# Token slots of an expert dealt out over eight groups of partitions, and a start at slot 4 in every second turn

## What is computed

```
x  = x + relu(segment_sum(edge_weight * (layernorm(x) @ W)[src], dst) + bias)
xt = layernorm(x)                                 # the input of the experts
scores = sigmoid(xt @ Wg.T + bg); w, idx = top_k(scores, 2); w = w / w.sum()
nx = layernorm(xt)
h  = silu(nx @ (gamma*W1) + b1') * (nx @ (gamma*W3) + b3')   # per expert, 64 of them
y  = sum over the token's two experts of w * (h @ W2 + b2)
z  = a small shared expert on nx
x  = x + y + z
```

## Time and profile before

| what | value |
|---|---|
| median of 3 runs | 431.51 us (431.15 to 432.36) |
| profiled execution, its own time | 432.0 us |
| its span in the profile | 430.2 us |
| PE busy | 398.4 us |
| plain transfers (q1) | 120.45 MB |
| transfers with an index per row (q0) | 8.28 MB |

### The profile page before, as it was taken

One profiled execution on the slowest core, in us unless ns is written; L12 is line 12 of the kernel. 1 busy time (PEld: TensorE's weight loads), 2 busy tenths in 40 slices (PEclk: granted clock), 3 DMA queues, 4 the chain that ended last, 5 costly groups with the idle time before them and its releaser, 6 DMA issues.

```text
span 430.2 us, 6405 instructions
## 1 busy us (share of the span) xinstructions
PE 398.4 (93%) x1898; PEld 207.4 (48%) x1899; DVE 213.2 (50%) x696; ACT 156.9 (36%) x387; POOL 174.1 (40%) x275
## 2 busy tenths in 40 slices
PE   6988999999999998999999999999898969897985
PEld 5656777756556557443443443443333433343331
DVE  8899998225666776633323323423313232123337
ACT  8767787322322220232332332332312321131232
POOL 2769996314655576523423323323312132121100
PEclk9999999999999998999999999999989998899999
DMA  7899971400002764499999999999999999999578
GB/s 254 211 335 408 406 287 47 137 31 26 25 25 63 281 232 146 151 402 410 400 407 405 410 406 407 406 407 406 405 406 409 405 408 404 406 399 406 231 273 325
DMA packets 44022, 129.15 MB, mean 300 GB/s; under 512 B 8054, under 2 KB 9270, under 8 KB 43858
## 3 DMA queue, kind: packets, MB, share of 16 engines
q1 hardware_dynamic: 38242, 120.45, 73.1%
q0 software_dynamic: 5744, 8.28, 5.4%
HBM read 119.64 MB, written 17.85 MB: 320 GB/s over the span
## 4 chain that ended last, share of the span: by engine, by line
PE 80%; issue 6%; DVE 5%; POOL 4%; DMA 3%; ACT 1%; SPq 1%; DVEq 0%; POOLq 0%; ACTq 0%
PE bank L1479 27%; PE bank L1342 13%; PE bank L1509 12%; PE bank L1501 5%; PE bank L1291 4%; PE bank L1467 4%; PE bank L1264 3%; DMA w<-totals 2%; PE bank L1236 2%; PE bank L1330 2%; PE bank L1363 2%; POOL M L502 1%; POOL AT L502 1%; PE bank L1351 1%; PE bank L1412 1%
## 5 line engine op out<-in xcount | busy, mean ns | idle before, releaser
L1136 DVE SCALAR_TENSOR_TENSOR osl<-bank,b13T,osl 128x64 f32<-128x64 f32 x128 | 27.5, 277 | 155.3 <-ACT osl L736 155.3
L1479 PE MATMUL bank<-w,xhT 128*64 128x512 f32 x368 | 87.6, 618 | 11.5 <-issue 11.5
L729 ACT COPY xh<-bank 128x512 f32<-128x512 f32 x33 | 19.4, 586 | 138.0 <-PE bank L1479 131.9
L1342 PE MATMUL bank<-HW,AT 128*128 128x512 f32 x128 | 58.2, 593 | 0.0
L1479 PEld LDWEIGHTS bank<-w,xhT 128*64 128x64 f32 x368 | 26.5, 141 | 56.5 <-issue 54.8
L596 POOL DMA_INDIRECT totals<-osl,A x16 | 16.4, 1028 | 80.2 <-PE bank L1467 72.1
L596 POOL DMA_INDIRECT totals<-GW,A x16 | 16.4, 1025 | 77.9 <-PE bank L1467 63.7
L1509 PE MATMUL bank<-w,osl 128*64 128x512 f32 x184 | 43.7, 593 | 1.6 <-DVE osl L1136 1.6
L592 POOL DMA_INDIRECT A<-nx_rows,A x33 | 34.3, 1039 | 12.3 <-issue 9.7
L1342 PEld LDWEIGHTS bank<-HW,AT 128*128 128x128 f32 x128 | 22.9, 191 | 21.0 <-issue 21.0
L645 ACT ACTIVATE osl<-iota,eT 128x128 f32<-128x128 f32 x90 | 27.8, 388 | 9.9 <-PE bank L1291 9.9
(11 more groups left out here) (238 smaller groups left out, 589.2 us busy)
## 6 DMA issues: line engine op xcount, KB each, us to landing
w<-in_L_ffn_W_dram SPq DMA_DIRECT2D x69, 1024.0 KB
A<-in_L_ffn_W_dram SPq DMA_DIRECT2D x15, 1024.0 KB
HW<-in_L_ffn_W_dram SPq DMA_DIRECT2D x8, 1024.0 KB
totals<-w SPq DMA_DIRECT2D x1, 4096.0 KB, 25.8
AT<-in_L_ffn_W_dram SPq DMA_DIRECT2D x4, 1024.0 KB
w<-totals SPq DMA_DIRECT2D x8, 512.0 KB, 7.4
out_dram<-X SPq DMA_DIRECT2D x8, 256.0 KB, 2.3
X<-in_x_dram SPq DMA_DIRECT2D x3, 512.0 KB, 9.5
```

The lines of the kernel that those rows point to most:

```text
L1136: ins = v.scalar_tensor_tensor(hT[b][:, m, CAP * h:CAP * h + CAP], bank[4][:, (HC + m) * P + CAP * h:(HC + m) * P + CAP * h + CAP], b13T[: ...
L1342: ins = t.matmul(bank[4 + s % 2][:, :], AT[:, s % 2, k, :], HW[:, k, :], start=(k == 0), stop=(k == NB - 1))
L1479: ins = t.matmul(bank[2 + b][CAP * h:CAP * h + CAP, :], xe[b][:, c, CAP * h:CAP * h + CAP], up_w[v][:, h, :, c, :], start=(c == 0), stop=( ...
```

## The change

Three things are altered. (1) Slot 32q + 8r + e of an expert no longer is partition 32q + 8r + e of its half but partition 32q + 4e + r: slots are dealt out one by one over eight groups of four partitions (e = 0 to 7). For the lists from memory ACT copies `L` into `Lspread` in that order and PE reads that; for blocks 5 to 7 `place` compares with a row `slot_of`, made by POOL, in place of `iota`. (2) `C` starts at 4 in place of 0 for the experts of turns with an odd pair number, so their lists begin at slot 4. (3) `count`, which decides on more passes, is that same `C`.

```diff
+SKIP = 4
+        slot_of = GW[:, 1, 448:512]
+        Lspread = xg[XG - 1][0:PAIRS, 2 * CAP * REC:4 * CAP * REC].rearrange("j (a p) -> j a p", a=REC)
...
+            g.iota(slot_of.rearrange("p (q e r) -> p q e r", q=2, e=8), pattern=[[CAP // 2, 2], [1, 8], [8, 4]], base=0,
+                   channel_multiplier=0, allow_small_or_imprecise_dtypes=True).then_inc(slot_of_ready, 1)
...
+            def spread_list():
+
+                act.wait_ge(list_in, 16)
+                slots_in = Lflat.rearrange("j (q r e a) -> j a q e r", q=4, r=4, e=8)
+                for i in range(REC):
+                    a.copy(Lspread[:, i, :].rearrange("j (q e r) -> j q e r", q=4, e=8), slots_in[:, i]).then_inc(list_spread, 1)
...
             for s in range(NB + 2):
+                if s == NB:
+                    spread_list()
...
-            v.memset(C, 0.0).then_inc(edges_ready, 1)
+            c_c = mark(v.memset(C, 0.0))
+            need(c_c)
+            v.memset(C[0:1, :].rearrange("p (j e) -> p j e", e=4)[:, :, 2:4], float(SKIP)).then_inc(edges_ready, 1)
...
-                    v.tensor_tensor(place[i], iota[:, 0:64].unsqueeze(1).broadcast_to([P, 2, 64]),
+                    v.tensor_tensor(place[i], slot_of.unsqueeze(1).broadcast_to([P, 2, 64]),
...
-                pe.wait_ge(list_in, 16)
+                pe.wait_ge(list_spread, REC)
                 for a in range(REC):
-                    t.matmul(list_bank[:, PAIRS * a:PAIRS * a + PAIRS], Lflat[:, a:a + REC * (P - 1) + 1:REC], ident[0:PAIRS, 0:PAIRS],
+                    t.matmul(list_bank[:, PAIRS * a:PAIRS * a + PAIRS], Lspread[:, a, :], ident[0:PAIRS, 0:PAIRS],
```

More of the change, by code:

```diff
@@ L293, in moe_gnn @@
         xe_first = sem("xe_first")
+        list_spread = sem("list_spread")
+        slot_of_ready = sem("slot_of_ready")
         y_out = [sem(f"y_out{i}") for i in range(YS)]
@@ L1034, in rank @@
                     dve.wait_ge(list_ps, t - DRAM_BLOCKS - 1)
+                if t == DRAM_BLOCKS:
+                    dve.wait_ge(slot_of_ready, 1)
                 if t >= DRAM_BLOCKS:
-                    v.tensor_tensor(place[i], iota[:, 0:64].unsqueeze(1).broadcast_to([P, 2, 64]),
+                    v.tensor_tensor(place[i], slot_of.unsqueeze(1).broadcast_to([P, 2, 64]),
                                     pos.unsqueeze(2).broadcast_to([P, 2, 64]), ALU.is_equal).then_inc(place_ready, 1)
```

## The result

The changed kernel takes 427.41 us (median of 9 runs, 426.41 to 430.0), beside 431.48 us for the kernel before: ratio 0.9913, interval 0.9896 to 0.993. By the ratio that is 3.7 us (3.0 to 4.5) of 431.5. No further pass ran. 459 us was forecast, with a range from 450 us, so the forecast was wrong; what came is its rival without a pass, for which 428 us had been worked out.

What follows compares the result with a forecast made beforehand. PE sets the pace up to about 309 us, then the weights on full DMA engines. Span 430.2 + 29.3 (pass) + 1.8 (clock) - 3.5 (deal-out) = 457.8; the runs' median lies 1.3 higher: 459.1, forecast 459 us, range 450 to 468.

Steps and rivals of the forecast that it cites:

- rival without a pass: No expert of the odd turns has 61 to 64 tokens, so only the deal-out acts: 428 us, 422.6 to 431.5, chance 0.13.
- The step that failed: Reading single DMA packets for turn 20: 63 and 39 tokens, so the start at 4 forces a pass behind all turns.
- the 31 us: Added behind the last turn by one further pass: 29.3 us of serial work and 1.8 us for PE's slower clock.
- The chance: Chance 0.84 that the kernel gets slower, through a further pass; the pass as summed, with its bounds, had 0.79.
- The dealing: Experts' stage: evening out row-by-row transfers over the 16 DMA engines gains 3.5 us, range 0 to 9.
- The upper part of its range: Gain towards 9 us if each turn's surplus rows always met the same DMA engines; 8.9 us over some 25 turns.
- The small edits: `iota`, second memset, `place`'s row and ACT's two copies (0.5 to 0.6 us) lie in idle time: costed at nothing.
- The profile's signs: With a pass: 34 gathers, read back near 436 to 440. Deal-out: PE's waits 3 to 4 us lower. Wrong if 33 gathers.
- The price of a pass: Behind the last `down`, in series: read back 29.3 us later (lower end 26), plus 1.8 us for the clock (0 to 7).
- the gather's landing: In the pass, from the gather's issue until its rows land: 3.03 us, taken from the scatter.
- The other terms: In the pass: until the gather's issue 4.08 us; PE's work 10.85, hand-overs 1.0 and clock 1.8; scatter 3.80.

Runs made afterwards that it cites:

- slot 5: The changed kernel with lists of the odd turns starting at slot 5 instead of 4 (`SKIP = 5`): 428.64 us, ratio 0.9924, no further pass.
- slot 6: The changed kernel with lists of the odd turns starting at slot 6 instead of 4 (`SKIP = 6`): 484.51 us, ratio 1.1224, two passes behind the last turn.
- one pass: The changed kernel with only the lists of experts 38 and 39 (turn 20) moved to slot 6, forcing a pass behind the last turn: 461.66 us, ratio 1.067.
- dealing alone: The changed kernel with every list starting at slot 0 (`SKIP = 0`): 429.26 us, ratio 0.9937.
- by twos: The changed kernel with slots dealt out two at a time, so two rows still lie side by side: 429.48 us, ratio 0.9962.
- four starts: The changed kernel with list starts 0, 4, 6 and 2 over every four pairs in place of two starts: 428.17 us, ratio 0.9926.
- start alone: The kernel before with only the start at slot 4 added, slots staying in order in their partitions: 432.21 us, ratio 1.0007.
- crowding: The changed kernel with eight slots in a row sent to one group of four partitions, and four half-size ACT copies: 443.25 us, ratio 1.0265.
- the 60 turns: The kernel with a forced pass for experts 38 and 39, plus 60 identity turns on PE while it waits for the gathered rows: 460.45 us, ratio 1.0646.
- with the next gap filled: The kernel with a forced pass for experts 38 and 39, plus 78 identity turns before the rows and 16 behind them; output spoiled: 459.04 us, ratio 1.0643.

## Why the prediction was wrong

**The step that failed** is "For the gather of turn 20 (experts 38 and 39) seen together with the scatter of turn 15, which has 22 and 22 rows, only 63 and 39 fit the 16 engines". All of the 31 us hung on it. The runs with slots 5 and 6 show 59 as the largest count of the odd pairs; 59 + 4 = 63 fits.

How the reading went wrong can be seen with the packets of both kernels side by side. That gather and that scatter move 146 rows in both. With 63 tokens the list would reach to slot 66 now, past the 64 slots, and three of those rows would have moved out of the gather into a further pass, so 146 in both kernels already speaks against it. Their packets with a single row are 2 before and 26 after. With slots in order an expert has one such packet if its count is odd, and none if even, so before all that shows is how many counts of the four are odd. 63, 39, 22 and 22 pass that, and so do 59, 43, 34 and 10. The rest of the reading, which engine had which packet, can't be followed from what is on record: it was a chain through many packets that were set down one by one by their times, and it was called exact without a second reading that could contradict it. With the slots dealt out, the number of single rows depends on the counts themselves, and over all turns only 59 and 43 are left for turn 20. Turn 18's 59 and 50 hold. The gather of turn 17, seen with a scatter of 78 rows, moves 92 rows before and 96 now, so the further pass has 14 rows before and 18 now: there the skip of 4 did what the diff says.

**The chance** given to the pass, 0.84, was the other half of the error. Its only support was that reading, and "I keep some doubt" was worth more than 0.16: whether one of 15 pairs has its larger count within four particular numbers is open without a reading.

**What held.** The dealing: 3.5 us forecast, 3.7 measured, and by the way that was given: the last engine 4.7 us behind the mean of the completions, about 1 us of unevenness to remain. The table has 5.1 for that same trace, so the 4.7 was read a little low, and 1.7 for the changed kernel. The upper part of its range, up to 9 us, by which every turn's surplus counts in full, was rightly not taken. The small edits cost nothing that shows (ACT's two copies took 0.71 us instead of 0.5 to 0.6, in idle time). The rival without a pass was forecast at 428 us, with 427.41 measured. The profile's signs that were named for it (33 gathers) are the ones that came; PE's waits fell by 1.6 us and not by 3 to 4: their sum leaves out the slow `up`, of which there is one less, and behind a slow one the next wait is shorter.

**The price of a pass,** 29.3 + 1.8 us over a kernel without one, was near: one pass costs 461.66 beside 427.4, or by the ratios (1.067 - 0.9913) x 431.5 = 32.7 us. The term that was mis-sized is the gather's landing, 5.88 instead of 3.03 us. The other terms are off by 0.25 to 0.54 us, in both directions.

**What stays open.** The Trainium skill (DMA: Bandwidth & Descriptors, The descriptor swizzle) gives each engine four partitions of every 32, with eight engines for each 64, in a full transfer of 128. I took that as the count's base: the tokens per expert as the packets leave them open, a row for each filled slot, 0.08 us a row, over the transfers that end before the last weights. Worked out against measured (last landing behind the mean): changed 2.1 and 1.7 us, dealing alone 3.3 and 3.3, by twos 3.6 and 3.4, four starts 1.8 and 2.0, slot 5 2.5 and 2.1; but start alone 7.7 and 6.3, and before 9.3 and 5.1. The landings agree with that mapping where the surplus is small, and crowding by it costs 15 us. Why the kernel before is less uneven than worked out is open. So is whether the start at 4 gives anything: with the dealing the last engine is 1.7 us behind the mean instead of 3.3, but the 1 us of time is within the noise, and without the dealing it gave nothing.

## What to carry to other kernels

- Where transfers by index share the DMA engines with a saturated weight stream, look at the completions of one weight transfer: the last engine's distance from their mean bounds what evening out can win as long as the bytes stay (5.1 us here, of which 3.7 were won), and it is cheap to win by dealing rows out over groups of partitions, one by one rather than by blocks.
- When a forecast hangs on a number that decides between 0 and 30 us, a reading of it wants a second reading that could contradict it; without one, the chance stays near what the spread of the data gives. A shift of the number by one (slot 5, slot 6) is a sharp and cheap test.
- A start inside a fixed capacity takes from the capacity: at 4 of 64 this input has one slot to spare (59 + 4 = 63), and one expert with 61 tokens in an odd pair would cost 32.7 us for a gain of 1 at best.

## What the runs showed of the hardware

- An uneven load of the 16 DMA engines delays the others once it is large: with the last engine 5.1 us behind the mean the DMA rate from 300 to 350 us was 407 GB/s, as in the changed kernel, and the mean was in its place; with the slots crowded, the rate there was 390 GB/s (383 from 350 to 400 us) and even the mean came 7 us later.
- A single row of 2 KB in a packet costs little more than half of two: packets of 2052 bytes took 87 ns on average and those of 4096 bytes 163 ns, with 599 and 1493 of them from 190 to 400 us among the row-by-row transfers of the changed kernel.
- When PE stood still for 2.43 us behind the 60 turns (6.8 us), windows with a granted clock of 0.71 and then 0.50 followed, and `up` took 5.83 us instead of 3.67. After 1.49 us, with the next gap filled, the clock stayed at 1.00.
- With 1.5 MB of weights issued ahead of it and nothing else on the queues, the gather of 18 rows in the pass behind the last turn landed 5.9 us after its issue; the scatter of these rows, with nothing ahead of it, let the read back start 2.4 us after its issue.
